# Norm 4 taken row by row, with layer 2's first query and key projections placed between its later rows

## What is computed

```python
x = x + gb * _L1_ffn_ref(h, ...)                 # mixture of experts
...
h = _layernorm(x, axis=-1) * (1 + ca) + sa       # norm 4
x = x + ga * _L2_attn_ref(h, Wq, Wk, Wv, Wo, bo) # attention

def _layernorm(x, axis=-1, eps=1e-05):
    m = jnp.mean(x, axis=axis, keepdims=True)
    v = jnp.var(x, axis=axis, keepdims=True)
    return (x - m) / jnp.sqrt(v + eps)

# in _L2_attn_ref
q = apply_rope(split_heads(x @ Wq))
k = apply_rope(split_heads(x @ Wk))
sim = jnp.einsum('bid,bjd->bij', q, k) * scale
```

## Time and profile before

| | |
|---|---|
| median of three executions | 1405.4 us (1404.46 to 1411.82) |
| the profiled execution, its own time | 1395.94 us |
| its span, first to last instruction | 1394.1 us |
| TensorE busy | 1195.4 us (86%) |
| VectorE busy | 1006.4 us (72%) |
| ScalarE busy | 909.3 us (65%) |
| GpSimd busy | 578.4 us (41%) |
| mean granted TensorE clock | 0.937 of full speed |

### The profile page before, as it was taken

The page is one execution under the profiler, slowest core; times in us unless marked ns, Lnnn a source line. Parts: engine busy times, 40 slices in busy tenths (PEclk is TensorE's granted clock), DMA queues, the critical chain, the costliest instruction groups (busy, mean ns, idle before and its releaser), DMA issues.

```text
span 1394.1 us, 28067 instructions
## 1 busy us (share of the span) xinstructions
PE 1195.4 (86%) x10484; PEld 693.8 (50%) x10484; DVE 1006.4 (72%) x2420; ACT 909.3 (65%) x2161; POOL 578.4 (41%) x554
## 2 busy tenths in 40 slices
PE   7887048759999999999978999997888879898878
PEld 5333048724555555555434666653555534555543
DVE  3455842248889889899664999995788954788864
ACT  4664002227777777777777888874888853788862
POOL 1022037624444444444230222224778731778740
PEclk9997559968999999999999999998999999999999
DMA  9002107430000000000010000000000000000000
GB/s 331 4 0 61 58 15 239 137 110 0 1 2 1 1 1 0 1 1 1 29 78 1 2 2 2 2 2 33 2 2 2 2 1 0 2 1 2 2 2 30
DMA packets 20677, 40.68 MB, mean 29 GB/s; under 512 B 3859, under 2 KB 13595, under 8 KB 19902
## 3 DMA queue, kind: packets, MB, share of 16 engines
q1 hardware_dynamic: 18494, 37.14, 7.9%
q0 software_dynamic: 2048, 1.74, 0.5%
HBM read 33.17 MB, written 6.55 MB: 28 GB/s over the span
## 4 chain that ended last, share of the span: by engine, by line
PE 74%; DVE 9%; issue 6%; ACT 5%; POOL 4%; DMA 1%; SPq 0%; POOLq 0%; DVEq 0%; ACTq 0%
PE bank L1111 5%; PE bank L1124 5%; PE bank L1503 5%; PE bank L1491 5%; PE pair L1082 5%; PE bank L1481 4%; PE bank L1509 4%; PE bank L1098 3%; PE pair L1098 3%; PE bank L2260 3%; PE pair L1085 2%; PE pair L1740 2%; PE pair L1995 2%; PE bank L1975 2%; PE bank L1131 2%
## 5 line engine op out<-in xcount | busy, mean ns | idle before, releaser
L1332 POOL TENSOR_TENSOR rope_part<-rope_part,rope_tab 128x512 f32<-128x512 f32 x64 | 81.4, 1272 | 195.1 <-DVE rope_part L1251 195.0
L1183 ACT ACTIVATE soft<-bank,neg_max 128x512 f32<-128x512 f32 (+2 forms) x192 | 100.5, 536 | 27.9 <-DVE neg_max L1259 27.7
L2198 POOL TENSOR_TENSOR win_part<-win_part,scaled_tab 128x512 f32<-128x512 f32 x64 | 81.7, 1277 | 81.0 <-DVE win_part L2134 80.6
L1556 POOL TENSOR_TENSOR win_soft_alibi<-win_soft_alibi,win_inv_alibi 128x384 f32<-128x384 f32 x64 | 51.6, 826 | 147.9 <-DVE win_inv_alibi L1540 147.8
L1195 ACT ACTIVATE softT<-bank 128x512 f32<-128x512 f32 x160 | 92.5, 599 | 30.7 <-PE bank L1111 30.6
L1098 PE MATMUL bank<-k_rope,q_rope 64*128 64x512 f32 (+3 forms) x384 | 97.3, 479 | 1.6 <-POOL k_rope L1337 1.6
L1259 DVE CUSTOM_DVE_ANT_0 bank<-bank,att_mask 128x512 f32<-128x512 f32 (+2 forms) x192 | 92.2, 522 | 6.9 <-PE bank L1098 6.9
L1516 ACT ACTIVATE win_soft_local<-bank,win_neg_max_local,rq 128x128 f32<-128x128 f32 x256 | 92.7, 477 | 0.0
L1111 PE MATMUL bank<-ident,soft 128*128 128x128 f32 x640 | 89.5, 279 | 0.6 <-ACT softT L1195 0.5
L277 POOL TENSOR_SCALAR h<-ln_norm,mod 128x512 f32<-128x512 f32 x28 | 24.3, 866 | 155.7 <-DVE ln_norm L261 155.7
L1275 DVE TENSOR_SCALAR soft<-soft,exp_inv 128x128 f32<-128x128 f32 (+2 forms) x160 | 87.5, 594 | 1.1
(11 more groups left out here) (406 smaller groups left out, 3383.0 us busy)
## 6 DMA issues: line engine op xcount, KB each, us to landing
moe_w<-in_moe_w SPq DMA_DIRECT2D x8, 960.0 KB, 5.4
y_tok<-in_moe_w SPq DMA_DIRECT2D x8, 960.0 KB, 5.1
y_dram<-zeros SPq DMA_DIRECT2D x8, 256.0 KB
htok_dram<-htok SPq DMA_DIRECT2D x2, 1024.0 KB
y_tok<-y_dram SPq DMA_DIRECT2D x8, 256.0 KB, 4.8
att_w<-in_att_w SPq DMA_DIRECT2D x1, 1536.0 KB, 7.6
att_w<-in_local_w SPq DMA_DIRECT2D x1, 1536.0 KB, 9.6
wmod<-in_wmod SPq DMA_DIRECT2D x1, 1152.0 KB, 7.4
```

The source lines that it names most:

```text
L1183: nc.scalar.activation(soft[par][:, hd, TILE_AT[t]:TILE_AT[t] + keys(t)], score_bank(u, s, hd)[:, at:at + keys(t)], ACT.Exp, scale=-1.0, b ...
L1332: nc.gpsimd.tensor_tensor(rope_part[2 * piece + 1][:, :], rope_part[2 * piece + 1][:, :], rope_tab[:, 2 * piece + 1, :], ALU.mult).then_in ...
L1556: nc.gpsimd.tensor_tensor(a["soft"][u % 2][:, js, :], a["soft"][u % 2][:, js, :], a["inv"][:, u % 2, js].unsqueeze(2).to_broadcast([128, 4 ...
L2198: nc.gpsimd.tensor_tensor(swapped, swapped, scaled_tab[:, 2 * j + 1, :], ALU.mult) \
```

## The change

Norm 4 gets functions of its own on TensorE, ScalarE and VectorE. Its rows use banks 1, 2, 4 and 1, so that bank 0 is free for the projections. A row is squared, averaged and rooted before the next one is squared. TensorE makes the query of unit 0 between rows 1 and 2 and the key between the centring and the variance of row 3; VectorE's two rope steps stand between its rows in the same way. GpSimd scales rows 2 and 3 after unit 0's rope. The wait for the whole norm moves to the first scores. A second load of the same ScalarE table ahead of the attention is left out.

```diff
@@ ln_bank
             if 20 <= n < 28:
                 return bank[(n - 20) % 3 if n < 24 else 0][:, :]
+            if 16 <= n < 20:
+                return bank[(1, 2, 4, 1)[n - 16]][:, :]
@@ att_scores
             if s == 0:
                 pe.wait_ge(sem("roped"), 4 * u + 4)
+                if u == 0:
+                    pe.wait_ge(sem("ln_normed"), 20)
@@ new
+        def norm4_pe(pe):
+
+            moe_out_pe(pe, 0)
+            moe_out_pe(pe, 1)
+            ln_centred(pe, 4, 0)
+            ln_variance(pe, 4, 0)
+            moe_out_pe(pe, 2)
+            ln_centred(pe, 4, 1)
+            ln_variance(pe, 4, 1)
+            moe_out_pe(pe, 3)
+            pe.wait_ge(sem("att_w_loaded"), 32)
+            att_project(pe, 0, 0)
+            ln_centred(pe, 4, 2)
+            ln_variance(pe, 4, 2)
+            ln_centred(pe, 4, 3)
+            att_project(pe, 0, 1)
+            ln_variance(pe, 4, 3)
+
@@ att_pe
-            pe.wait_ge(sem("ln_normed"), 20)
-            pe.wait_ge(sem("att_w_loaded"), 32)
...
-                if project:
+                if project and u > -2:
                     att_project(pe, u + 2, 0)
...
-                if project:
+                if project and u > -2:
                     att_project(pe, u + 2, 1)
@@ ScalarE
+        def norm4_act(act):
+            nc.scalar.preload_act_table_set("natural_log_exp_and_others")
+            for b in range(B):
+                ln_squared(act, 4, b)
+                ln_root(act, 4, b)
+
         def att_act(act):
-            nc.scalar.preload_act_table_set("natural_log_exp_and_others")
@@ VectorE
+        def norm4_dve(dve):
+            moe_sums_dve(dve, 0)
+            for b in range(1, B):
+                moe_sums_dve(dve, b)
+                moe_add_dve(dve, b - 1)
+            ln_normed(dve, 4, 0)
+            moe_add_dve(dve, B - 1)
+            ln_normed(dve, 4, 1)
+            dve.wait_ge(sem("att_tables"), 32)
+            att_rope(dve, 0, 0)
+            ln_normed(dve, 4, 2)
+            att_rope(dve, 0, 1)
+            ln_normed(dve, 4, 3)
+
...
-                if project:
+                if project and u > -2:
                     att_rope(dve, u + 2, 0)
@@ GpSimd, att_pool (ln_pool(pool, 4) ahead of it is taken out)
+            ln_scaled(pool, 4, 0)
+            ln_scaled(pool, 4, 1)
             pool.wait_ge(sem("att_tables"), 32)
             for u in range(UNITS):
                 rope(u, 0)
                 rope(u, 1)
+                if u == 0:
+                    ln_scaled(pool, 4, 2)
+                    ln_scaled(pool, 4, 3)
```

More of the change, by code:

```diff
@@ L1294, in att_dve @@
             link(dve, "dve", nc.vector.tensor_scalar(gate_bo[:, :], mod[:, 2, 2, :], v("attn2_bo"), None, ALU.mult))
-            dve.wait_ge(sem("att_tables"), 32)
             for u in range(-2, UNITS + 1):
@@ L2378, in _ @@
             moe_pool(pool)
-            ln_pool(pool, 4)
             att_pool(pool)
@@ L2400, in _ @@
             moe_act_engine(act)
-            ln_act(act, 4)
+            norm4_act(act)
             att_act(act)
@@ L2428, in _ @@
             moe_dve(dve)
[L2430 to L2440, removed]
+            norm4_dve(dve)
             att_dve(dve)
@@ L2473, in _ @@
             moe_pe(pe)
[L2475 to L2480, removed]
+            norm4_pe(pe)
             att_pe(pe)
```

## The result

The changed kernel took 1401.24 us (median of 12, 1393.33 to 1408.84) against 1410.36 us for the kernel before (median of 12, 1402.66 to 1414.72), run beside each other. The ratio is 0.9944 with a 95% interval of 0.9921 to 0.9967, so about 7.9 us less (0.56% of 1410; the two medians by themselves differ by 9.1). The forecast was 1399.0 us, 6.4 us less than the 1405.4 of three executions; twelve executions put the kernel before at 1410.4.

The account below looks back on a forecast made before the run. Between norm 4 and the first scores TensorE mostly waits in a serial chain, with an unsteady clock. Gains of 3.6 (6.1 less 2.5), 1.35 and 1.5 make 6.4 us: 1405.4 to 1399.0 us, range 1394.5 to 1405.

Parts of the forecast that it names:

- The key's path at full clock: Norm 4 to unit 0's scores: with TensorE at full clock, scores start at 305.6 instead of 311.74, gaining 6.1 us.
- The half clock ahead of it: TensorE in norm 4: clock still at half speed for row 0, costing 2.5 us of the 6.1 gained.
- the hole: TensorE's 0.7 us wait for ScalarE between row 0's centring and variance, claimed to delay the clock's rise, costing 2.5 us.
- signs against it: Profile signs of a wrong forecast: clock rise at 291.2 (more gained) or behind 300 (less gained).
- Behind the first scores: From unit 0's scores to unit 1's: full instead of half clock gains 1.35 us.
- The dip at unit 1's scores: Half-clock stretch 321.9 to 328.6 before: less likely after the change, gain 0 to 2.5 us, taken as 1.5.
- likeliest stretch: Whole kernel: the forecast's own values, 1397 to 1402 us, likeliest 1399.0, chance 0.57.
- edits at nothing: Around the attention's start: table load, norm wait, GpSimd scalings and other small edits stay hidden, costing or gaining nothing.
- A: Rival at norm 4: clock rises as early as before, no second dip; gain 9.95 us, 1395.4 to 1398.3, chance 0.20.
- B: Rival at norm 4: clock rises only among rows 1 to 3; 0 to 3 us left, or loss 1.8; chance 0.15.
- C: Rival: half clock from 291 past the attention's start, slower by more than 0.5%, 6.8 us, 1412; chance 0.03.
- D: Rival at the attention's start: something unnamed gives the gain back later, time stays 1404.4 to 1405.9; chance 0.05.

Follow-up runs that it names:

- third profile: Changed kernel profiled again with nothing altered, on the same chip as the kernel before with the hole put in; ratio to the kernel before 0.9924 (0.9901 to 0.9947).
- filler: Changed kernel plus one unread 192-column TensorE product between row 0's centring and variance; no ratio, first scores at 14.97 us, unit 2's at 38.58.
- counter-experiment: Kernel before with rows 0 and 1's variances right behind their centrings on TensorE; no ratio, clock rise at 0.6 us, first scores at 22.36.

## Why the prediction was right, and where it wasn't

**The key's path at full clock** was a walk to 305.6, that is 15.2 us behind the first squaring. The third profile of the changed kernel, with its rise at 0.2, has 14.95. The pitches were 3.3 and 4.2; it shows 3.1 (293.42 to 296.53 for the variances) and 4.0. Gain by the sum 6.1, measured 21.32 - 14.95 = 6.4.

**The half clock ahead of it** was charged with 2.5 us, for a rise within the run behind the hole. The measured charge is 1.9 us at a rise of 4.5 (16.84 - 14.95), 4.0 at 9.7 and 0 at 0.2. As an amount 2.5 was in the middle; as a step it failed. The prediction had named as signs against it a rise at 291.2 or one behind 300, which are 0.8 and 9.6 us behind the first squaring. The third profile has the rise even sooner than the one, the first profile just behind the other, and only the one with its rise at 4.5 has it where it was forecast, past 291.2 and before 296. I took the clock to rise within a run of 5.1 us without a hole. In the first profile that run is there, variance, transposes and centring from 306.69 to 311.32, and the clock did not rise in it. TensorE then waited again, for row 1's squaring, a hole that I had not counted; the rise came 3.7 us into the next run, at 315.7. The cause I gave, the hole of row 0, isn't shown to be the cause.

**Behind the first scores** 1.35 us was right: 28.42 - 18.99 = 9.43 us from unit 0 to unit 1 against 10.68, so 1.25.

**The dip at unit 1's scores** was the mis-sized term. I gave it 0 to 2.5 and took 1.5. Where there is no dip, unit 1 to unit 2 takes 11.17 or 11.18 (six profiles), with one 14.09 to 14.18 (seven); it costs 2.9 to 3.0 us. The changed kernel had none in the first two profiles and in the one with the table load, and a shorter one in the third (12.68). My reason, that a clock which has been full for longer dips less, isn't borne out: filler had full clock from 0.1 on and dipped, and the changed kernel dipped with its rise at 0.2 and not with those at 4.5 and 9.7. Why the clock dips in one execution and not in another stays open. With the waits for the key filled there was no dip in the one profile taken.

**Sum.** At unit 2's scores the three profiles of the change lead the first of before by 6.5, 8.7 and 9.1 us, against 6.4 forecast and 7.9 measured by the ratio. In the first profile the agreement is partly luck: its first scores gained 2.3 us and not 3.6, and the missing dip gave back 2.9 and not 1.5, so the two misses of 1.3 and 1.4 cancel. The absolute 1399.0 against 1401.24 has luck in it too: the base was 5.0 us too low and the gain 1.5 us (by the ratio) to 2.7 (by the medians) too small, and the two offset each other in part. And the edges of the likeliest stretch were reckoned from 7.1 and 4.6, where the prediction's own terms give 3.6 + 1.35 + 2.5 = 7.45 and 4.95; neither edge moves by more than 0.35 us. Of the edits at nothing, the table load was measured and is nothing. The scalings on GpSimd, moved behind the key, ended 1.5 us after it at 326.5, before unit 1's rope. The new wait for the whole norm was met at 324.09 against 325.03. That the gain passes through is seen in the earlier trace rows and after alike, 11.6 us per unit.

**The rivals.** A (an early rise) happened in one of three profiles, though with a short dip; B (half clock for longer) had its condition met in the first: the rise, at 315.7, lies among the rows, between the squarings of rows 1 and 2 (311.36 and 317.15), and the 2.3 us left at the first scores are within its 0 to 3. But 4.2 us more came behind them, for which B had no room. C and D did not happen.

## What to carry to other kernels

Where a norm ends in a serial chain of projection, rotation and scores, start the first projection as soon as its own row is ready: here the kernel with the row order alone was 3.4 us late at the first scores in its profile, and with the early projections it led by 6 to 9 at unit 2's. Compare profiles from an event at the start of the changed stretch and not from zero, since an unchanged stage upstream moved by 15 us between profiles, mostly from chip to chip. And where an engine's granted clock moves within the stretch, take several profiles before giving a cause for where it rose or fell: two profiles of the change fitted my story, and the third and a counter-experiment didn't.

## What the runs showed that was not expected

The three chips differ by 1.1% for the same program (medians of the kernel before 1411.3, 1395.8 and 1397.3 us); the first squaring lay at 304.7 to 307.6 us in the four profiles of the first and at 288.6 to 295.6 in the eight of the others. By its first squaring (290.42) and its time (1395.94 us) the profile of the kernel before fits the second group, and that of the changed kernel (306.04) the first; on which chips the two were taken isn't on record.

A small VectorE instruction, `gate_bo` on 128x4 elements, took 0.22 us before, while GpSimd was idle, and 1.00 us after the change, while GpSimd ran `k_rope` (323.71, 1.26 us) and the scalings:

```profile
324.00 1.00 DVE L1333 TENSOR_SCALAR gate_bo<-mod,vec 128x4 f32<-128x4 f32 x1
324.96 1.52 POOL L279 TENSOR_SCALAR h<-ln_norm,mod 128x512 f32<-128x512 f32 x2
```

It lies off the path. The other profiles repeat this: in the four in which it ran clear of GpSimd's products it took 0.22 us, in the ten in which one ran beside it 0.67 to 1.30, and in each of the ten it ended 0.02 to 0.03 us behind the end of that product. `k_rope` itself took 1.26 us either way, so it was VectorE that was held up; why was not tried.

The last stages, which the change doesn't touch, differed as well: from unit 2's scores to the end took 1394.1 - 336.53 = 1057.6 us before and 1397.1 - 345.64 = 1051.5 after. So the 3.0 us between the two spans are 15.6 more ahead of norm 4, 6.5 less in the changed stretch and 6.1 less behind it.
